# Eight small stages of an attention layer as one stage

## The chip, the cores and the metric

One core of one Trainium2 chip runs the whole program in one launch. The time is that of the device in microseconds (us): 6660.32, the median of three runs (6659.06 to 6661.24). Engines: TensorE (PE), VectorE (DVE), ScalarE (ACT), GpSimd (POOL), and SyncE (SP), which here only issues DMAs.

## The reference, cut to what matters

The program is a network of eight layers over 3125 nodes with 256 features. The change lies in the seventh, a graph layer with two paths. The attention path and the state-space ("mamba") path are both normalised and then mixed by a gate:

```
agg = segment_sum(proj[src] * attn, tgt)            # attention, 4 heads of 64
h_local = elu(agg + x + gat_b)
h_local = layer_norm(h_local, ln_local_g, ln_local_b)
y = scan(...)                                        # state space, in the order of perm
y = (y + xc * D_param) * silu(z)
y = y @ out_proj_w.T
h_attn = layer_norm(x + y[inv], ln_global_g, ln_global_b)
gate = sigmoid(h_local @ wl.T + h_attn @ wg.T)
h = gate * h_local + (1 - gate) * h_attn
```

Here `x` is the layer's normalised input. `elu(v)` is computed as `max(v, 0) + exp(min(v, 0)) - 1`.

## The kernel before, in words

**Sizes.** 3200 padded nodes are NT = 25 tiles of P = 128 rows, in NG = 5 groups of G = 5. D = 256 is KD = 2 halves of 128. Buffers with nodes on the partitions ("rows") are [128, 25, 256]; buffers with features on the partitions ("turned") are [128, 2, 3200], worked on in NCH = 8 chunks of CH = 400 nodes. All is float32. A buffer of rows has 3.28 MB (3200 KB).

**Stages.** The program is a sequence of stages. Each is a `Phase` (L53): it takes semaphores and buffers, has one program per engine, and ends with a barrier of all engines that clears its semaphores (L87). Nothing of the next stage is issued before it. Within a stage each engine's program is in order; a `wait_ge` holds everything behind it on that engine. SP's DMAs go through one queue.

**Around the change** (`attention_layer`, L3290). After `mamba_and_attention`, whose VectorE does the scan, the scan's output stands turned in `k.t` (buffer `t_sb`), the attention's sums in `k.ag` (buffer `y_sb`, 260 columns per tile, the last four the sums of the weights), the layer's input in DRAM. Then come, each a stage:

1. `gz`, `gate_rows` (L2293): SP loads the kept rows into `x_sb`, then z chunk by chunk through two buffers; ScalarE applies Silu, VectorE multiplies into `k.t`.
2. `tm`, `transform` with mode "rows" (L1147): ScalarE copies a tile of `k.t`, TensorE multiplies by `out_proj_w`, VectorE evacuates, SP stores to the DRAM table `ys`. G buffers each.
3. `lr`, `local_rows` (L2355): a chain of eight operations on one partition, with an Exp of ScalarE and a product of TensorE in it, gives a small number per tile that is added to the sums; then reciprocal, scaling, the two additions (input, `gat_b`) and elu, each as one instruction over all 6400 columns (the scaling one per head).
4. `nl`, `affine_norm` (L2156): statistics, mean and root; then three VectorE operations per tile (subtract and scale, times gain, plus bias). SP reloads a kept buffer meanwhile.
5. `tl`, `turn` (L2217): VectorE copies a tile, TensorE transposes both halves, ScalarE copies out of PSUM to the turned buffer.
6. `fr`, `fetch_rows` (L2328): GpSimd gathers rows of `ys` by the inverse permutation (`k.rank`), five buffers; VectorE copies the index, and adds the kept rows.
7. `ng`: `affine_norm` again, 8. `tt`: `turn` again, into `t2`.

The gate stage `gf` (`gate_and_feed`, L2412) then loads its weights and works on `k.t` and `t2` in chunks. It isn't touched, nor is what comes after, but for `affine_norm` of the last norm (`n2g`), which loses two options that it doesn't use.

## Time and profile before

| | us |
|---|---|
| median of 3 runs | 6660.32 |
| the profiled execution, its time | 6658.88 |
| the same, span in the trace | 6657.1 |
| TensorE matmul busy in the span | 5195.0 (78%) |
| VectorE busy | 3514.9 (53%) |
| ScalarE busy | 2499.8 (38%) |
| GpSimd busy | 1679.7 (25%) |
| mean granted clock of TensorE | 0.877 of full |

Shares are of the whole span, over stages with quite different limits; what a change to one stage is worth is read from that stage. The time is 1.8 us more than the span: the launch around it. A row of a timeline gives a group's start and length from the span's start, the engine, the line, the operation with its output and inputs, and in brackets how long the engine was idle before it and what ended that.

### The profile page before, as it was taken

To read this page: it belongs to the slowest core of one execution; us is meant where nothing else is said; L and a number is where in the kernel's file an instruction comes from. 1 tells how busy PE (TensorE), PEld (TensorE's weight loads), DVE (VectorE), ACT (ScalarE), POOL (GpSimd) and SP (SyncE) were. 2 spreads that over 40 slices of the span, in tenths; PEclk is the share of its full clock that TensorE was granted. 3 is DMA by queue.
4 is the path that set the end of the run, shared out by engine and by line. 5 is a ranking of instruction groups with operands and counts; after the bars stand their busy time and mean duration, and the time that the engine had idled before them with its cause. 6 is when DMAs were issued, how large, how long until landed. Compare 5 with 4: busy or idle time off the path is not lost. (4 is left out here: it accounts for less than half of the span.)

```text
span 6657.1 us, 91573 instructions
## 1 busy us (share of the span) xinstructions
PE 5195.0 (78%) x22747; PEld 3550.6 (53%) x22748; DVE 3514.9 (53%) x7704; ACT 2499.8 (38%) x5918; POOL 1679.7 (25%) x1614
## 2 busy tenths in 40 slices
PE   6939998999796999998999497674756666326886
PEld 3516664444584777766788375463334444213476
DVE  9837777778553444443000334324489999664111
ACT  7947774666230000002223000232456565311343
POOL 5877770000011000001111300144334444010012
PEclk9979998999798999998999799786767777668888
DMA  1113333333363222220356421365234444310055
GB/s 30 23 20 99 102 101 111 151 150 152 114 198 90 70 71 70 73 63 30 112 188 197 131 71 38 102 198 164 68 95 134 135 134 135 84 47 2 26 153 170
DMA packets 407368, 682.81 MB, mean 103 GB/s; under 512 B 72610, under 2 KB 304813, under 8 KB 406573
## 3 DMA queue, kind: packets, MB, share of 16 engines
q1 hardware_dynamic: 328684, 490.20, 22.9%
q0 software_dynamic: 74016, 186.25, 10.3%
q10 hardware_dynamic: 4512, 4.46, 0.2%
q8 instruction: 78, 1.28, 0.1%
q14 instruction: 78, 0.63, 0.0%
HBM read 511.42 MB, written 169.02 MB: 102 GB/s over the span
## 5 line engine op out<-in xcount | busy, mean ns | idle before, releaser
L1784 POOL DMA_INDIRECT e_xb<-table,source x188 | 180.7, 961 | 2383.7 <-issue 1925.1
L1099 DVE TENSOR_TENSOR a_diff<-a_cu 128x640 f32<-128x640 uint16 x480 | 396.2, 825 | 628.0 <-PE a_pa L1137 628.0
L995 PE MATMUL ty_pc<-ty_ohr,ty_ohl 128*128 128x512 bf16 (+1 forms) x3416 | 661.2, 357 | 2.5 <-DVE ty_ohl L934 2.5
L2629 POOL DMA_INDIRECT mx_at_rows<-heads,mx_at_ix x416 | 483.6, 1162 | 617.4 <-PE mx_at_pa L2675 514.6
L1137 PE MATMUL a_pa<-a_diff,y_sb 128*128 128x320 f32 (+1 forms) x2000 | 549.0, 435 | 63.4 <-DVE a_diff L1106 63.4
L1762 DVE TENSOR_TENSOR e_ys<-e_py,e_bl 128x256 f32<-128x256 f32 x188 | 79.9, 425 | 970.4 <-PE e_py L1711 970.4
L1741 ACT ACTIVATE e_h<-e_phid,e_b 128x256 f32<-128x256 f32 (+1 forms) x760 | 333.1, 438 | 689.0 <-PE e_phid L1699 671.6
L969 ACT CAST ty_new<-ty_pc 128x512 uint16<-128x512 f32 x854 | 449.8, 542 | 265.2 <-PE ty_pc L995 265.2
L1699 PE MATMUL e_phid<-e_xt,e_w 128*128 128x256 f32 (+1 forms) x2800 | 526.2, 346 | 2.9 <-ACT e_xt L1729 2.9
L1711 PE MATMUL e_py<-e_wl,e_h 128*128 128x256 f32 x2288 | 512.4, 379 | 0.0
L995 PEld LDWEIGHTS ty_pc<-ty_ohr,ty_ohl 128*128 128x128 bf16 x3416 | 314.0, 98 | 349.8 <-DVE ty_ohl L934 4.2
L1137 PEld LDWEIGHTS a_pa<-a_diff,y_sb 128*128 128x128 f32 (+1 forms) x2000 | 379.6, 191 | 225.9 <-DVE a_diff L1106 63.8
L1699 PEld LDWEIGHTS e_phid<-e_xt,e_w 128*128 128x128 f32 x2800 | 464.1, 194 | 54.1 <-issue 4.9
L1068 ACT COPY t_sb<-a_pa 128x320 f32<-128x320 f32 x80 | 34.1, 426 | 1146.5 <-PE a_pa L1137 1140.3
L2675 PE MATMUL mx_at_pa<-mx_at_rows,mx_at_oh 128*128 128x260 f32 x832 | 298.2, 481 | 206.4 <-DVE y_sb L2613 145.9
L1711 PEld LDWEIGHTS e_py<-e_wl,e_h 128*128 128x128 f32 x2288 | 424.9, 190 | 55.4 <-ACT e_h L1741 0.4
L748 POOL DMA_INDIRECT a_rows<-table,a_ix x416 | 403.6, 970 | 153.4 <-issue 121.6
L2696 ACT ACTIVATE mx_at_rows<-mx_at_rows 128x64 f32<-128x64 f32 x1664 | 406.9, 334 | 0.0
L815 PEld LDWEIGHTS a_pa<-a_oh,a_rows 128*128 128x128 f32 x1664 | 249.1, 193 | 200.2 <-issue 187.3
L1137 PE MATMUL a_pa<-a_diff,a_xs 128*128 128x320 f32 (+1 forms) x1000 | 276.6, 436 | 98.9 <-DVE a_diff L1106 98.9
L235 PE MATMUL a_ss_sums<-a_ss_tiles,a_ss_lanes 125*128 125x416 f32 x800 | 348.1, 516 | 6.3 <-ACT a_ss_tiles L228 6.3
L333 POOL DMA_INDIRECT rec<-es_recs,es_tgt x240 | 312.2, 1301 | 131.6 <-issue 130.7
(611 smaller groups left out, 8992.4 us busy)
## 6 DMA issues: line engine op xcount, KB each, us to landing
counts<-ty_snap SPq DMA_DIRECT2D x122, 800.0 KB, 3.3
a_cu<-counts SPq DMA_DIRECT2D x500, 160.0 KB, 2.2
mx_work<-bc SPq DMA_DIRECT2D x160, 320.0 KB, 3.6
e_w<-in_L_ffn_W SPq DMA_DIRECT2D x33, 1024.0 KB
e_wl<-in_L_ffn_W SPq DMA_DIRECT2D x32, 1024.0 KB, 7.9
e_wl<-in_L_ffn_Wd SPq DMA_DIRECT2D x32, 1024.0 KB, 5.7
ybuf<-e_ys POOLq DMA_DIRECT2D x78, 256.0 KB
e_w<-in_L_ffn_w SPq DMA_DIRECT2D x16, 1024.0 KB
```

Source lines behind the costliest of these rows:

```text
L235: mm = pe.matmul(self.sums[:, 0:ST], self.lanes[:, b, j, :], self.tiles[:, b, j, :], start=False, stop=False)
L333: g.indirect_dma_start(rec, bass.IndirectOffsetOnAxis(ap=tgt[:, c:c + 1], axis=0), recs[:, c, :], None).then_inc(placed[c // HALF % 2].sem ...
L748: g.indirect_dma_start(rows[:, j, :], None, table, bass.IndirectOffsetOnAxis(ap=ix[:, j:j + 1], axis=0)).then_inc(landed[j].sem, 16)
L969: a.copy(new[:, u % 2, q * WIDE:q * WIDE + w], pc[:, q, 0:w]).then_inc(taken, 1)
L995: mm = pe.matmul(pc[:, q, 0:w], ohl[:, h, j, ts(q, P)], ohr[:, h, j, 0:w], start=j == 0, stop=j == ROWS - 1)
L1099: v.tensor_tensor(diff[:, m % DIFFS, :], cu[:, s % R, :], cu[:, (s - 1) % R, :], ALU.subtract).then_inc(done, 1)
L1137: mm = pe.matmul(pa[:, q, 0:H], xs[l % 2][0:rows, s, ts(q // 2, P)], diff[0:rows, m % DIFFS, ts(q % 2, H)], start=s == 0, stop=s == NT - 1)
L1699: mm = pe.matmul(phid[:, (offs[l] + f) % NB, 0:size], ws[l][:, sl, q, f * P:(f + 1) * P], src, start=q == 0, stop=q == kt - 1)
L1711: mm = pe.matmul(py[:, (s * NR + n) % 2, 0:D], hs[-1][:, q, n * P:(n + 1) * P], wls[:, s, q, :], start=q == 0, stop=q == KL - 1)
L1741: a.activation(hs[l][:, f, :], phid[:, (offs[l] + f) % NB, 0:size], hidden[l][2], bias=bs[l][:, sl, f:f + 1]).then_inc(hact, 1)
L2629: g.indirect_dma_start(self.rows[:, h * STEP + j, :], None, self.table, bass.IndirectOffsetOnAxis(ap=self.ix[:, h, j:j + 1], axis=0)).then ...
L2696: ins = a.activation(part, part, ACT.Identity, scale=self.rows[:, j, D + q:D + q + 1])
```

## The change

The eight stages become one, `join_paths`, written out without loops. What each engine does in it:

- **SP** loads z through three buffers, then `out_proj_w`; it stores projected tiles as they come, and issues the load of the kept rows in five groups once the last z load and fifteen stores are issued. The other kept buffer is reloaded last.
- **VectorE** does the small chain, then the eight products with z with the scaling of the attention's sums (per group of five tiles) between them; then the additions and elu per group, with the statistics of each group at once; the subtraction and scaling of the first norm in place; then per fetched tile the addition and the statistics; then the second norm. Gain and bias are not applied here.
- **TensorE** multiplies straight from `k.t` (no copy), two PSUM buffers; transposes straight from the normalised rows in pairs of tiles, four PSUM buffers.
- **ScalarE** does Silu, evacuates the projection into five buffers, computes for elu `Relu(-v)` and `Exp(-that)` per group, the roots, and writes the transposed halves to `k.t` and `t2` with `Identity`, gain as scale and bias as bias, from two [128, 1] columns in SBUF: a turned row has its feature on the partition.
- **GpSimd** loads the small vectors, waits for all stores, then gathers with ten buffers and takes its index from `k.rank` directly.

```
+def join_paths(nc, k, w, lists, zs, kept, ys, refill, t2):
+    F, own, ZR, RG, SLOTS = D // HEADS, lists[3], 3, 10, 4
+    groups = [slice(g * G, g * G + G) for g in range(NG)]
+    pairs = [range(t, min(t + 2, NT)) for t in range(0, NT, 2)]
+    rows, held = k.rows, k.x
+        begun, risen, powered, told, chain, scaled = (ph.sem(n) for n in ("begun", "risen", "powered", "told", "chain", "scaled"))
+        bb, inv, low = ph.sb("bb", [P, D]), ph.sb("inv", [P, NT, HEADS]), ph.sb("low", [P, 2, G, D])
+        z, wsb, out = ph.sb("z", [P, ZR, KD, CH]), ph.sb("w", [P, KD, D]), ph.sb("out", [P, G, D])
+        fetched, st = ph.sb("fetched", [P, RG, D]), ph.sb("st", [P, NT, 6])
+        pb, pz, pt = ph.ps("pb", [P, 512]), ph.ps("pz", [P, 2, 512]), ph.ps("pt", [P, SLOTS, 2, KD, P])
...
             @b.sync
             def _(sp):
+                for c in range(ZR):
+                    sp.dma_start(z[:, c, :, :], zs[:, :, c * CH:(c + 1) * CH]).then_inc(zld[c], 16)
+                sp.dma_start(wsb[:, :, :], w("out_proj_w").rearrange("(k p) n -> p k n", p=P)).then_inc(wld, 16)
+
+                def store(tiles):
+                    for t in tiles:
+                        sp.wait_ge(put, t + 1)
+                        sp.dma_start(ys[ts(t, P), :], out[:, t % G, :]).then_inc(stored[t % G], 16)
+
+                ends = [max(c - ZR + 1, 0) * CH // P for c in range(NCH)]
+                for c in range(ZR, NCH):
+                    sp.wait_ge(mixed, c - ZR + 1)
+                    sp.dma_start(z[:, c % ZR, :, :], zs[:, :, c * CH:(c + 1) * CH]).then_inc(zld[c % ZR], 16)
+                    store(range(ends[c - 1], ends[c]))
+                for g, s in enumerate(groups):
+                    sp.dma_start(held[:, s, :], kept[:, s, :]).then_inc(yld[g], 16)
+                store(range(ends[-1], NT))
+                sp.wait_ge(scaled, NG)
+                sp.dma_start(k.y, refill).then_inc(refilled, 16)
+                sp.wait_ge(refilled, 16)
...
+            @b.gpsimd
...
+                for s in stored:
+                    g.wait_ge(s, 16 * NG)
+                for t in range(NT):
+                    if t >= RG:
+                        g.wait_ge(attended, t - RG + 1)
+                    g.indirect_dma_start(fetched[:, t % RG, :], None, ys, bass.IndirectOffsetOnAxis(ap=k.rank[:, t:t + 1], axis=0)).then_inc(landed[t % RG].sem, 16)
...
             @b.vector
...
+                def mix(i):
+                    v.wait_ge(silu, i + 1)
+                    part = k.t[:, :, i * CH:(i + 1) * CH]
+                    v.tensor_tensor(part, part, z[:, i % ZR, :, :], ALU.mult).then_inc(mixed, 1)
+
+                def share(g):
+                    s = groups[g]
+                    v.tensor_tensor(rows[:, s, :].rearrange("p t (h f) -> p t h f", h=HEADS), k.ag[:, s, 0:D].rearrange("p t (h f) -> p t h f", h=HEADS),
+                                    inv[:, s, :].unsqueeze(3).broadcast_to([P, G, HEADS, F]), ALU.mult).then_inc(scaled, 1)
+
+                def local(g):
+                    s = groups[g]
+                    v.wait_ge(scaled, g + 1)
+                    v.wait_ge(yld[g], 16)
+                    c(v.tensor_tensor(rows[:, s, :], rows[:, s, :], held[:, s, :], ALU.add))
+                    v.tensor_tensor(rows[:, s, :], rows[:, s, :], bb[:, :].unsqueeze(1).broadcast_to([P, G, D]), ALU.add).then_inc(biased, 1)
+
+                def bend(g):
+                    s = groups[g]
+                    v.wait_ge(bent, g + 1)
+                    v.wait_ge(biased, g + 1)
+                    c(v.scalar_tensor_tensor(rows[:, s, :], rows[:, s, :], 0.0, low[:, g % 2, :, :], ALU.max, ALU.add))
+                    v.tensor_scalar(rows[:, s, :], rows[:, s, :], -1.0, None, ALU.add).then_inc(joined, 1)
+                    v.wait_ge(joined, g + 1)
+                    for t in range(g * G, g * G + G):
+                        v.bn_stats(st[:, t, :], rows[:, t, :]).then_inc(stats, 1)
+
+                def spreads(n):
...
+                    v.sem_inc(varied, 1)
+                    v.wait_ge(rooted, n + 1)
+                    c(v.reciprocal(rstd[:, n, :], rstd[:, n, :]))
+
+                def even(n, buf):
+                    for t in range(NT):
+                        v.tensor_scalar(buf[:, t, :], buf[:, t, :], mean[:, n, t:t + 1], rstd[:, n, t:t + 1], ALU.subtract, ALU.mult).then_inc(evened, 1)
+
                 v.wait_ge(told, 1)
+                c = Chain(v, chain)
+                mix(0)
+                c(v.tensor_tensor(inv[:, :, :], k.ag[:, :, D:D + HEADS], spread(pb[:, 0:NT], HEADS), ALU.add))
                 c(v.reciprocal(inv[:, :, :], inv[:, :, :]))
+                for i in range(1, NCH):
+                    mix(i)
+                    if i <= NG:
+                        share(i - 1)
+                v.wait_ge(vld, 16 * 5)
+                for g in range(NG):
+                    local(g)
+                    if g:
+                        bend(g - 1)
+                bend(NG - 1)
+                spreads(0)
+                even(0, rows)
+                for t in range(NT):
+                    landed[t % RG].wait(v, 16 * (t // RG + 1))
+                    v.tensor_tensor(held[:, t, :], held[:, t, :], fetched[:, t % RG, :], ALU.add).then_inc(attended, 1)
+                    v.wait_ge(attended, t + 1)
+                    v.bn_stats(st[:, t, :], held[:, t, :]).then_inc(stats, 1)
+                spreads(1)
+                even(1, held)
...
             @b.tensor
...
+                pe.wait_ge(wld, 16)
+                for t in range(NT):
+                    pe.wait_ge(mixed, (t * P + P - 1) // CH + 1)
+                    if t >= 2:
+                        pe.wait_ge(put, t - 1)
+                    for q in range(KD):
+                        mm = pe.matmul(pz[:, t % 2, 0:D], k.t[:, q, ts(t, P)], wsb[:, q, :], start=q == 0, stop=q == KD - 1)
+                    mm.then_inc(mul, 1)
+                for n, buf in enumerate((rows, held)):
+                    for m, tiles in enumerate(pairs):
+                        i = n * len(pairs) + m
+                        pe.wait_ge(evened, n * NT + tiles[-1] + 1)
+                        if i >= SLOTS:
+                            pe.wait_ge(evac, KD * (i - SLOTS + 1))
+                        for j, t in enumerate(tiles):
+                            for q in range(KD):
+                                mm = pe.transpose(pt[:, i % SLOTS, j, q, :], buf[:, t, ts(q, P)], k.ident[:, :])
+                        mm.then_inc(tdone, 1)
...
             @b.scalar
...
+                def bright(i):
+                    a.wait_ge(zld[i % ZR], 16 * (i // ZR + 1))
+                    a.activation(z[:, i % ZR, :, :], z[:, i % ZR, :, :], ACT.Silu).then_inc(silu, 1)
+
+                def take(t):
+                    a.wait_ge(mul, t + 1)
+                    if t >= G:
+                        a.wait_ge(stored[t % G], 16 * (t // G))
+                    a.copy(out[:, t % G, :], pz[:, t % 2, 0:D]).then_inc(put, 1)
+
+                done = 0
+                for i in range(NCH):
+                    bright(i)
+                    for t in range(done, i * CH // P):
+                        take(t)
+                    done = max(done, i * CH // P)
+                for t in range(done, NT):
+                    take(t)
+                for g, s in enumerate(groups):
+                    a.wait_ge(biased, g + 1)
+                    if g >= 2:
+                        a.wait_ge(joined, g - 1)
+                    a.activation(low[:, g % 2, :, :], rows[:, s, :], ACT.Relu, scale=-1.0).then_inc(negated, 1)
+                    a.wait_ge(negated, g + 1)
+                    a.activation(low[:, g % 2, :, :], low[:, g % 2, :, :], ACT.Exp, scale=-1.0).then_inc(bent, 1)
+                for n, dest in enumerate((k.t, t2)):
+                    a.wait_ge(varied, n + 1)
+                    a.activation(rstd[:, n, :], var[:, n, :], ACT.Sqrt).then_inc(rooted, 1)
+                    a.wait_ge(vld, 16 * 5)
+                    for m, tiles in enumerate(pairs):
+                        i = n * len(pairs) + m
+                        a.wait_ge(tdone, i + 1)
+                        for q in range(KD):
+                            cols = dest[:, q, tiles[0] * P:(tiles[-1] + 1) * P].rearrange("p (t c) -> p t c", c=P)
+                            a.activation(cols, pt[:, i % SLOTS, 0:len(tiles), q, :], ACT.Identity, scale=gains[:, n, q:q + 1], bias=biases[:, n, q:q + 1]).then_inc(evac, 1)
...
-        gate_rows(nc, k, zs, y_kept)
-        transform(nc, "tm", k, k.t, w("out_proj_w"), "rows", table=ys)
-        k.x, k.y = k.y, k.x
-        k.rows = sb("rows", [P, NT, D])
-        local_rows(nc, k, by_dst, w("gat_b"))
-        affine_norm(nc, "nl", k, k.rows, w("ln_local_g"), w("ln_local_b"), k.rows, False, refill=x_kept)
-        turn(nc, "tl", k, k.t, rows=k.rows)
-        fetch_rows(nc, k, ys)
-        affine_norm(nc, "ng", k, k.rows, w("ln_global_g"), w("ln_global_b"), k.rows, False)
         with nc.sbuf_tensor("t2", [P, KD, NP], F32) as t2:
-            turn(nc, "tt", k, t2, rows=k.rows)
+            with nc.sbuf_tensor("rows", [P, NT, D], F32) as k.rows:
+                join_paths(nc, k, w, by_dst, zs, y_kept, ys, x_kept, t2)
+            k.x, k.y = k.y, k.x
             gate_and_feed(nc, k, t2, w("wl"), w("wg"), w("ff1_w"), w("ff1_b"), w("ff2_w"), w("ff2_b"))
         turn_back(nc, "tb", k, k.t, k.y)
-        affine_norm(nc, "n2g", k, k.y, w("ln2_g"), w("ln2_b"), k.x, True)
+        affine_norm(nc, "n2g", k, k.y, w("ln2_g"), w("ln2_b"), k.x)
...
-_L3_BY_PARTITION = ("conv_b", "dt_proj_b", "D_param", "ff1_b", "ff2_b")
+_L3_BY_PARTITION = ("ln_local_g", "ln_local_b", "ln_global_g", "ln_global_b", "conv_b", "dt_proj_b", "D_param", "ff1_b", "ff2_b")
```

The small chain at the start of VectorE's program, left out above, is that of `local_rows` (L2372 to L2382). The statistics in `spreads` are those of `affine_norm` (L2181 to L2187).

## Rows read from the trace of the kernel before

**Rows 1.** Table of windows: length, each engine's busy us (instructions), clock, DMA share, GB/s.
```profile
5704.10:5953.60 249.50, 41.03 (x202) 35.77 (x202) 158.25 (x373) 46.48 (x93) 23.64 (x25) 0.58 0.21 69
...
5739.50:5769.50 30.00, 23.91 (x100) 20.43 (x100) 10.62 (x25) 9.74 (x25) 0.00 (x0) 0.88 0.34 118
```

**Rows 2.** Timeline at the stretch's start: start, us, engine, line, operation.
```profile
5703.64 0.43 DVE L2613 TENSOR_TENSOR y_sb<-y_sb,mx_at_pa 128x260 f32 x1 [0.21 <-PE mx_at_pa L2675]
5705.18 0.34 SPq L2309 DMA_DIRECT2D x_sb<-y_kept  x1
```

**Rows 3.** Timeline of the stage `lr` (local_rows).
```profile
5770.05 0.19 DVE L2372 CAST lr_first<-d_own 1x52 f32<-1x52 int32 x1 [3.06 <-PEq L87]
...
5776.20 0.22 ACT L2407 ACTIVATE lr_gap<-lr_gap 1x25 f32<-1x25 f32 x1 [4.90 <-DVE lr_gap L2379]
...
5777.47 0.26 DVE L2385 TENSOR_TENSOR lr_inv<-y_sb,lr_pb 128x100 f32<-128x100 f32 x1 [0.77 <-PE lr_pb L2402]
...
5778.57 7.03 DVE L2388 TENSOR_TENSOR rows<-y_sb,lr_inv 128x1600 f32<-128x1600 f32 x4
...
5792.50 6.83 DVE L2393 TENSOR_TENSOR rows<-rows,lr_bb 128x6400 f32<-128x6400 f32 x1
5799.36 3.49 DVE L2394 TENSOR_SCALAR lr_low<-rows 128x6400 f32<-128x6400 f32 x1
5802.89 5.54 ACT L2409 ACTIVATE lr_low<-lr_low 128x6400 f32<-128x6400 f32 x1 [26.47 <-DVE lr_low L2394]
```

**Rows 4.** The tile gz_z, by line: ns min/median/max.
```profile
L2305 ACT ACTIVATE gz_z<-gz_z x8: 869/869/870, 5716.8 to 5736.8; 128x800 f32<-128x800 f32 x8
L2325 DVE TENSOR_TENSOR t_sb<-t_sb,gz_z x8: 991/993/993, 5717.8 to 5737.8; 128x800 f32 x8
```

**Rows 5.** Timeline of the stage `tm` (transform, "rows").
```profile
5742.61 23.91 PE L1202 MATMUL tm_pz<-tm_w,tm_ast 128*128 128x256 f32 x100 [39.13 <-DMA tm_w<-in_L_gnn_out_proj_w]
...
5744.80 0.42 DVE L1226 COPY tm_out<-tm_pz 128x256 f32<-128x256 f32 x1 [6.03 <-PE tm_pz L1202]
```

**Rows 6.** A window of 2 us in the stage `nl`, columns as rows 1.
```profile
5826.00:5828.00 2.00, 0.00 (x0) 0.00 (x0) 2.00 (x7) 0.00 (x0) 0.00 (x0) 0.50 0.98 422
```

**Rows 7.** Timeline: statistics of `nl`; straight code of a refresh stage.
```profile
5820.31 8.27 DVE L2177 BATCH_NORM_STATS2 nl_st<-rows  x25 [1.42 <-PEq L87]
...
4492.90 0.17 DVE L1977 TENSOR_TENSOR c_mean<-c_st 128x5 f32<-128x5 f32 x1
...
4494.91 1.71 DVE L1968 TENSOR_SCALAR y_sb<-x_sb,c_mean,c_rstd 128x256 f32<-128x256 f32 x5
```

**Rows 8.** Timeline of the stage `fr` (fetch_rows), then its gathers by tile.
```profile
5869.92 0.94 POOL L2341 DMA_INDIRECT fr_rows<-ys,fr_ix  x1 [195.89 <-DVE fr_ix L2346]
...
5872.84 0.42 DVE L2350 TENSOR_TENSOR rows<-fr_rows,x_sb 128x256 f32 x1 [3.53 <-DMA fr_rows<-ys,fr_ix]
5873.41 0.15 DVE L2352 COPY fr_ix<-rank 128x1 uint32 x1
...
L2341 POOL DMA_INDIRECT fr_rows<-ys,fr_ix x25: 942/946/947, 5869.9 to 5899.9; - x25
```

**Rows 9.** Timeline of `tt` and `gf`, then two tiles of `gf`.
```profile
5943.36 7.12 PE L2250 MATMUL tt_pt<-ident,tt_stage 128*128 128x128 f32 x40 [76.06 <-DVE tt_stage L2238]
5944.19 8.51 ACT L2258 COPY t<-tt_pt 128x256 f32 x25 [29.30 <-PE tt_pt L2250]
...
5953.56 0.38 SPq L2427 DMA_DIRECT2D gf_wl<-in_L_gnn_wl  x1
...
5966.54 1.28 ACT L2471 ACT_TABLE_LOAD   x1 [13.85 <-PE gf_pg L2440]
...
L2477 ACT ACTIVATE gf_hid<-gf_ph,gf_b x32: 594/595/595, 5974.7 to 6092.1; 128x400 f32<-128x400 f32 x32
...
L2471 ACT ACTIVATE gf_gate<-gf_pg x16: 504/504/505, 5967.8 to 6081.3; 128x400 f32<-128x400 f32 x16
```

**Rows 10.** From the page's groups, the attention's gathers beside VectorE's scan.
```profile
L2629 POOL DMA_INDIRECT mx_at_rows<-heads,mx_at_ix x416 | 483.6, 1162 | 617.4 <-PE mx_at_pa L2675 514.6
```

More of the change, by code:

```diff
@@ L2153, in _, with affine_norm @@
                 a.activation(var[:, :], var[:, :], ACT.Sqrt).then_inc(root, 1)
-def affine_norm(nc, name, k, src, gain, bias, dest, add, eps=1e-5, refill=None):
+def affine_norm(nc, name, k, src, gain, bias, dest, eps=1e-5):
     with Phase(nc, name) as ph:
         ld, dve, root = ph.sem("ld", "hardware"), ph.sem("dve"), ph.sem("root")
-        filled = ph.sem("filled", "hardware")
         st = ph.sb("st", [P, NT, 6])
@@ L2168, in _ @@
                 sp.dma_start(bb[:, :], bias.partition_broadcast(P)).then_inc(ld, 16)
-                if refill is not None:
-                    sp.dma_start(k.x, refill).then_inc(filled, 16)
-                    sp.wait_ge(filled, 16)
             @b.vector
@@ L2190, in _ @@
                 v.wait_ge(ld, 32)
-                n, m = c.n, 4 if add else 3
+                n, m = c.n, 4
                 with v.Fori(0, NG) as i:
@@ L2386, in _ @@
                 c(v.reciprocal(inv[:, :, :], inv[:, :, :]))
-                for h in range(HEADS):
-                    v.tensor_tensor(k.rows[:, :, h * F:(h + 1) * F], ag[:, :, h * F:(h + 1) * F], spread(inv[:, :, h], F), ALU.mult).then_inc(dve, 1)
-                c.n += HEADS
-                v.wait_ge(dve, c.n)
-                c(v.tensor_tensor(k.rows[:, :, :], k.rows[:, :, :], k.y[:, :, :], ALU.add))
-                v.wait_ge(ld, 16)
-                c(v.tensor_tensor(k.rows[:, :, :], k.rows[:, :, :], bb[:, :].unsqueeze(1).broadcast_to([P, NT, D]), ALU.add))
@@ L2394, in _ @@
-                c(v.tensor_scalar(low[:, :, :], k.rows[:, :, :], 0.0, None, ALU.min))
-                v.wait_ge(act, 1)
-                c(v.scalar_tensor_tensor(k.rows[:, :, :], k.rows[:, :, :], 0.0, low[:, :, :], ALU.max, ALU.add))
-                c(v.tensor_scalar(k.rows[:, :, :], k.rows[:, :, :], -1.0, None, ALU.add))
+                for i in range(1, NCH):
[3 more added lines that the diff above has]
+                v.wait_ge(vld, 16 * 5)
```

227 lines of the change are left out of this document (28 added, 199 removed).

## The prediction

> **What bounds the kernel now.** I read the table of windows first, then the timeline of the stretch, then single tiles. The eight stages that the change merges run from the end of VectorE's last scan operation (5703.64 + 0.43 = 5704.07) to the first DMA of the gate stage at 5953.56: 249.5 us [rows 1, 2, 9]. In them VectorE works 158.3 us, ScalarE 46.5, TensorE 41.0, GpSimd 23.6 [rows 1]; their sum is 269 us, hardly more than the stretch, so the engines take turns. No wait between two neighbouring stages can be hidden, as each stage ends in a barrier. The rest of the kernel (gate stage, last norm) isn't touched, so the question is how long one merged stage takes. I lay it out along VectorE, with time zero at its release, 1.1 us after 5704.07 (SP's first DMA came at 5705.18, [rows 2]).
>
> **The change part by part, along VectorE.**
>
> *Opening, to 10.7.* The small chain on the softmax's tops stays: 5770.05 to 5777.47, 7.4 us [rows 3]. Z's first load now goes ahead of the 3.2 MB of kept rows and has landed by then. But ScalarE is in order: its Exp stood at +6.15 (5776.20), then comes the table load for Silu, 1.28, and a Silu of 0.87 [rows 3, 4, 9]. So the first product starts at 8.6 (1.2 us late), takes 1.0, and the inverse of the sums 1.1 (5777.47 to 5778.57) [rows 3, 4].
>
> *Eight products with z, five shares, projection beside them, to 30.6.* VectorE alone would need 7 x 1.03 + 5 x 1.5 = 14.7 (a share is 1280 elements; the four old ones had 1600 in 1.76 each [rows 3]), to 25.4. I don't think it gets that. ScalarE's program places three evacuations between one Silu and the next, and each waits for TensorE: the old projection took 23.91 us for 25 tiles, the first of them out after 2.2 (5742.61 to 5744.80), so 0.9 each after it [rows 5]. First product done 9.7, first tile 11.9, two more at the clock that TensorE has after idling (mean 0.88 of full over that old stage [rows 1]) 14.7, evacuation 0.4, the third Silu ends at 16.0. Then five rounds of 3 x 0.9 bring the eighth Silu to 29.5 and its product to 30.6. What the old stage paid for copying the operand (25 ScalarE copies) and VectorE's evacuations vanish from VectorE.
>
> *Local rows, to 73.4.* Per group of five tiles: two additions of 1280 elements, 1.5 each (6400 took 6.83), then the maximum-add 1.5, the minus one 0.8 (6400 took 3.49), and five statistics of 0.33 with a wait, 1.8: 3.0 + 4.1 [rows 3, 7]. That is 35.5 for five groups. The separate minimum of 3.49 and the 5.54 of Exp that VectorE waited for [rows 3] go. What is late next is ScalarE again: the first bend needs Relu and Exp, and they are queued behind the last seven evacuations. SP puts five loads of kept rows (3.28 MB) into its queue at about 26, ahead of the stores of tiles 15 to 24. At 422 GB/s [rows 6] they take 7.8 us and, with some 2 us of latency, a store behind them lands at about 36.5. The ring of five output buffers makes evacuation 20 wait for store 15, so the last evacuation ends at 40.0; Relu 1.25 (a fifth of 5.54 and a start), table 1.28, Exp 1.25 make 43.9. VectorE, through with two groups' additions at 36.7, stands for 7.2 us. From there five bends (20.5) and three pairs of additions (9.0) bring it to 73.4. If stores were not held the wait would be 3.5, that is 3.7 less.
>
> *First norm, to 85.1.* From the last statistics to the scaling takes 2.1 in straight code (4492.90 to 4494.91, and 0.1 for the semaphore ahead), plus a table load for Sqrt, 1.3, which I take as exposed; at most that is gained. Then 25 subtract-and-scale operations at 0.33 (five in 1.71, each 0.41, overlapping) are 8.3 [rows 7]. The multiplications by gain and additions of bias, 50 VectorE operations, and 25 copies into a stage are gone. Transposes and ScalarE's 26 turned evacuations (13 us, below) lie beside the next loop.
>
> *Fetched rows, to 107.6.* The index copies go. Per tile: addition, its semaphore and the next start 0.57 (5872.84 to 5873.41), statistics 0.33: 0.90, 22.5 in all [rows 7, 8]. GpSimd issues a gather each 1.25 (5869.9 to 5899.9 in 24 steps, 0.946 of it busy) [rows 8], 2.9 from its start to VectorE's use. All 25 stores have landed by 42 to 44, and the first ten gathers are out 12.5 later, long before 85.1. The other fifteen wait for freed buffers: the last starts at 85.7 + 14 x 1.25 = 103.2 and is usable at 106.1, and VectorE gets to it at 106.7. It is nearly a tie; bounds of the loop are 18.8 (0.75 a tile, if the semaphore's time is hidden) and 31.3 (all gathers at GpSimd's pace).
>
> A rule of the Trainium skill bears on this (SBUF — State Buffer, "SBUF: two separate sides"): while VectorE holds the port pair that it shares with GpSimd, GpSimd cannot write its descriptors. The trace has gathers of 1162 ns beside a busy VectorE against 946 in the old fetch stage [rows 8, 10], so it shows a slowing by a quarter and no full block. By the rows a gather beside the bends costs 1.5 with its gap, ten 15 us, still hidden; by the rule as a full block they would start only in VectorE's gaps (a rival, below).
>
> *Second norm and the tail, to 124.0.* 2.1 again, no new table. Then VectorE runs 8.3, TensorE turns pairs of tiles (40 transposes in 7.12, 0.18 each, 0.72 a pair) and ScalarE writes them with gain and bias. This last one is dearer than the copy that it replaces. 25 old copies took 8.51, 0.34 each [rows 9]. A bias from memory cost 0.595 - 0.504 = 0.09 on the same shape [rows 9]; with a scale from memory too I take 0.17, which gives 0.5 each, 1.0 a pair (bounds: 0.34 if it's free, 0.6). So ScalarE is the bound: first pair after 1.5, twelve full pairs and a single tile 12.8, together 14.3. Exit to the gate stage 0.9 (5952.70 to 5953.56) [rows 9].
>
> *Off the path:* the vectors on GpSimd's queue (due at 30), the refill of 3.2 MB on SP after the last store (landed by 52), the first norm's transposes. Without cover the refill would cost 10 us.
>
> A second rule of the skill speaks against the change (ScalarE: Activation LUTs, "What ACT_TABLE_LOAD costs"): a load of 1283 ns is followed by a drain of 1380 ns. The trace has a load at 5966.54 for 1.28 and the first Sigmoid at 5967.8 [rows 9], so no drain. With it, the three loads that I count as exposed (Silu, Exp, Sqrt) would make the time about 4 us longer, 6541.
>
> **Sum.** 1.1 + 124.0 + 0.9 = 126.0 against 249.5: 123.5 less. The profiled execution had a span of 6657.1 and a time of 6658.88, so 6658.88 - 123.5 = 6535.4 in its terms. The median shown is 6660.32, 1.4 above it: 6536.8, given as 6537.
>
> **Rivals.**
> 1. *ScalarE never holds VectorE.* Products done at 25.4, rows at 60.9, norm at 72.8 (with 3.4 and 8.3), loop 95.3, then 2.1 and a tail of 10.9 with ScalarE at 0.34: 108.3, or 110.3 with the ends. Time 6660.3 - 139.2 = 6521. For it: ScalarE has only 46 us of work before. Against: evacuations and Silus stand in one order.
> 2. *Gathers become the bound.* If GpSimd gets no gather out before the loop (blocked by VectorE's wide operations, or the stores late by 40 us), the loop is 25 gathers at 1.25 to 1.46, 31 to 36.5, in place of 22.5: 9 to 14 longer, 6546 to 6551. Against: rows 10.
> 3. *TensorE stays at 1.2 GHz*, as it stands beside these stages (0.50 in [rows 6]), where I count on 2.4 GHz after the first tiles. A tile then takes 1.9: five rounds of 5.7 instead of 2.7, and seven tiles at the end 7 us more, less the hold by the stores (already over, 3.7): 15 + 7 - 3.7 = 18, 6555. Against: the old projection climbed within a few tiles once it ran without a pause [rows 1, 5].
> 4. *Slower than before: straight code.* The old stages were loops over five groups; the new one has some 185 VectorE operations written out. If each had to wait for its code, all of it would lie on the path; it decides from 123.5 / 185 = 0.67 us per operation, and at 0.75 the time is 6537 + 139 = 6676. Against: another straight stage runs five such operations in 1.71 [rows 7].
>
> **Chances.** My forecast 0.58 (own range 6528 to 6546), rival 1 0.13, rival 2 0.12, rival 3 0.09, rival 4 0.02; 0.06 for sums of small misses outside these. Same to within 0.2% (13 us, what a measurement of this kernel can tell) would need a stage of over 236 us: 0.01. Faster 0.97. The range takes in the forecast, the edge of rival 1 and rivals 2 and 3: 6522 to 6556.
>
> **What the changed profile would show.** The merged stage 126 us long. VectorE waiting for Silus some 5 us in all, one wait of about 7 for ScalarE before the first maximum-add, and nearly none for gathers. If it waits for DMA in the fetch loop, my tie fell the wrong way. ScalarE's turned evacuations at 0.5 us apart and bounding the end; if they are at 0.34, the tail is 3 to 4 shorter. A granted clock under 0.6 during the projection would be rival 3. The gate stage must take as long as before; if it doesn't, the prediction is wrong in a part that I left out.

## The result, and the profile after

The changed kernel takes 6541.20 us (median of four runs, 6540.17 to 6542.21) against 6660.78 for the one before: 119.6 us less, a ratio of 0.9819 (95% interval 0.9802 to 0.9837). The prediction was 6537, with a range of 6522 to 6556. The profiled execution took 6542.21, its span is 6540.4. Between the two profiled executions the span fell by 116.7 us (6657.1 to 6540.4): the merged stage gives 119.1, what stands ahead of it took 4.2 more (the scan ends at 5708.27, before at 5704.07), and what follows took 1.8 less. The gate stage itself, from its first DMA to the last norm's, is as long as before: 158.0 against 157.8.

The first view is the timeline of the merged stage, where it begins and ends (the rest of each line as in [rows 2]). The last VectorE operation of the scan ends at 5707.84 + 0.43 = 5708.27, the gate stage's first DMA is at 5838.71: 130.4 us, against 249.5 before [rows 1, 2, 9] and 126.0 forecast.

```profile
5707.84 0.43 DVE L2554 TENSOR_TENSOR y_sb<-y_sb,mx_at_pa 128x260 f32 x1 [0.21 <-PE mx_at_pa L2616]
5709.39 1.97 SPq L2170 DMA_DIRECT2D jp_z<-zs  x3
...
5715.59 0.22 ACT L2314 ACTIVATE jp_gap<-jp_gap 1x25 f32<-1x25 f32 x1 [10.40 <-DVE jp_gap L2213]
5715.83 1.28 ACT L2318 ACT_TABLE_LOAD   x1
...
5718.10 0.99 DVE L2221 TENSOR_TENSOR t_sb<-t_sb,jp_z 128x800 f32<-128x800 f32 x1 [2.01 <-ACT jp_z L2318]
```

```profile
5838.71 0.38 SPq L2368 DMA_DIRECT2D gf_wl<-in_L_gnn_wl  x1
```

The opening is as forecast: Exp, then the table load, then Silu, and the first product 8.7 after the release at 5709.39 (8.6 forecast). Compare [rows 2, 3].

The second view is the timeline from the last rounds, where ScalarE evacuates the projection between two Silus, to the first maximum-add.

```profile
5733.35 0.37 ACT L2324 COPY jp_out<-jp_pz 128x256 f32<-128x256 f32 x1 [1.54 <-DMA ys<-jp_out]
...
5736.79 3.12 SPq L2184 DMA_DIRECT2D x_sb<-y_kept  x5
...
5739.05 0.37 ACT L2324 COPY jp_out<-jp_pz 128x256 f32<-128x256 f32 x1 [0.91 <-DMA ys<-jp_out]
...
5739.96 16.83 SPq L2176 DMA_DIRECT2D ys<-jp_out  x10
...
5743.18 1.49 DVE L2232 TENSOR_TENSOR rows<-rows,x_sb 128x1280 f32<-128x1280 f32 x1 [1.97 <-DMA x_sb<-y_kept]
...
5750.92 0.71 ACT L2324 COPY jp_out<-jp_pz 128x256 f32<-128x256 f32 x2 [9.85 <-DMA ys<-jp_out]
...
5751.43 4.33 PE L2298 MATMUL jp_pz<-jp_w,t_sb 128*128 128x256 f32 x12 [8.88 <-ACT jp_out L2324]
5753.51 0.37 ACT L2324 COPY jp_out<-jp_pz 128x256 f32<-128x256 f32 x1 [1.88 <-PE jp_pz L2298]
...
5756.07 1.27 ACT L2338 ACTIVATE jp_low<-rows 128x1280 f32<-128x1280 f32 x1
...
5757.36 1.28 ACT L2340 ACT_TABLE_LOAD   x1
5758.65 1.27 ACT L2340 ACTIVATE jp_low<-jp_low 128x1280 f32<-128x1280 f32 x1
...
5759.95 1.49 DVE L2239 SCALAR_TENSOR_TENSOR rows<-rows,jp_low 128x1280 f32<-128x1280 f32 x1 [10.83 <-ACT jp_low L2340]
5760.29 2.14 POOL L2201 DMA_INDIRECT jp_fetched<-ys,rank  x1 [0.30 <-issue]
```

The reader is to see three things. Two evacuations (5733.35 and 5739.05) wait for a store, and then the first addition (5743.18) 1.97 us for kept rows. Evacuation 20 waits 9.85 us for the store of tile 15, which SP issued at 5739.96, behind the five loads of kept rows (5736.79). And VectorE stands 10.83 us before its first maximum-add, until ScalarE, behind its evacuations, is through with Relu (5756.07), a table load and Exp. The gathers run beside that (5760.29) and are told of below.

The third view is the rest of the stage, by the same columns: first norm, fetch loop, second norm and tail. It answers to [rows 7 to 9].

```profile
5783.59 1.28 ACT L2343 ACT_TABLE_LOAD   x1
...
5790.69 0.23 ACT L2343 ACTIVATE jp_rstd<-jp_var 128x25 f32<-128x25 f32 x1 [5.82 <-DVEq L2255]
...
5791.30 8.17 DVE L2261 TENSOR_SCALAR rows<-rows,jp_mean,jp_rstd 128x256 f32<-128x256 f32 x25
...
5799.37 0.43 DVE L2282 TENSOR_TENSOR x_sb<-x_sb,jp_fetched 128x256 f32<-128x256 f32 x1
...
5800.18 0.41 DVE L2282 TENSOR_TENSOR x_sb<-x_sb,jp_fetched 128x256 f32<-128x256 f32 x1
...
5815.97 0.43 DVE L2282 TENSOR_TENSOR x_sb<-x_sb,jp_fetched 128x256 f32<-128x256 f32 x1 [0.36 <-DMA jp_fetched<-ys,rank]
...
5817.16 0.42 DVE L2282 TENSOR_TENSOR x_sb<-x_sb,jp_fetched 128x256 f32<-128x256 f32 x1 [0.31 <-DMA jp_fetched<-ys,rank]
...
5824.07 8.17 DVE L2261 TENSOR_SCALAR x_sb<-x_sb,jp_mean,jp_rstd 128x256 f32<-128x256 f32 x25
...
5826.07 11.73 ACT L2350 ACTIVATE t<-jp_pt,jp_biases,jp_gains 128x256 f32<-128x256 f32 x26 [2.39 <-PE jp_pt L2308]
```

The scaling of 25 tiles takes 8.17. The fetch loop from 5799.37 to 5821.79 takes 22.4: 0.81 for its first tile (5799.37 to 5800.18), then 0.79 a tile, and 1.2 to 1.3 for the last six (5815.97 to 5817.16 is one), where each addition waits for its gather. ScalarE's 26 turned instructions take 11.73, 0.45 each, and end at 5837.80, where VectorE is through at 5832.24: ScalarE bounds the end, as forecast.

### The profile page after: what moved, and what is told of

Read it like the earlier page. It is cut to its first block and busy times, and to the rows that moved or that the text cites. A ratio compares the mean times of both kernels' runs of the same rounds, so it can differ in the third digit from the quotient of the medians.

```text
span 6540.4 us, 90176 instructions
## 1 busy us (share of the span) xinstructions
PE 5198.6 (79%) x22747; PEld 3549.0 (54%) x22748; DVE 3445.6 (53%) x7515; ACT 2507.4 (38%) x5926; POOL 1683.8 (26%) x1619
```

## The experiments

For all but e6 I compare the length of the merged stage, from the end of the scan's last VectorE operation to the gate stage's first DMA: the stages ahead of it are the same instructions in all these kernels, and yet the merged stage began up to 8.5 us apart (at 5705.91 in e5, at 5714.44 in e3), so that the time alone can't tell 2 us. Each length is that of one profiled execution. The change has 130.4, and 130.2 in a later run on another chip (e11); no other measure of the stage's own noise was taken. e1 to e4 ran on one chip, e5 to e8 on a second, e9 to e11 on a third.

### e1: ten output buffers

```
-        ph.sems("stored", G, "hardware")
+        ph.sems("stored", OUTS, "hardware")     # OUTS = 10
...
-        ph.sb("out", [P, G, D])
+        ph.sb("out", [P, OUTS, D])
```

> Ten output buffers instead of five between the projection's evacuations and their stores, nothing else. In the changed kernel the merged stage takes 130.4 us and VectorE waits 10.8 us for the first Exp. Theory A: ScalarE is held at evacuation 20 because its buffer's store stands behind the five loads of kept rows in SP's queue. With ten buffers evacuations 20 to 24 need only stores issued ahead of the loads; ScalarE is through by about 38 us into the stage instead of 47.9, the wait shrinks to 1 or less, the stage to 120 to 121, the time to 6531. Theory B: the wait is made by ScalarE's own Relu, table load and Exp (3.9 us) and by the late kept rows: then it stays at 7 or more and the time at 6538 to 6541.

Measured: stage 119.3 (5712.31 to 5831.6), time 6535.25 (6530.31 to 6538.88). Timeline of e1, evacuations and the first maximum-add:

```profile
5745.95 1.49 DVE L2233 TENSOR_TENSOR rows<-rows,x_sb 128x1280 f32<-128x1280 f32 x1 [1.61 <-DMA x_sb<-y_kept]
...
5748.32 0.37 ACT L2325 COPY jp_out<-jp_pz 128x256 f32<-128x256 f32 x1 [0.49 <-PE jp_pz L2299]
...
5752.89 1.49 DVE L2240 SCALAR_TENSOR_TENSOR rows<-rows,jp_low 128x1280 f32<-128x1280 f32 x1 [0.99 <-ACT jp_low L2341]
```

The last evacuation starts at 5748.32, 36.0 after the scan's end (47.5 in the change), and VectorE's wait is 0.99 in place of 10.83. Theory A holds, B falls: of the 10.8 nearly all was the ring of five buffers behind the queue's order. The time came out 4 above the forecast 6531; in the profiled execution the merged stage began 4.0 us later than the change's.

### e2: the stores ahead of the kept rows

```
-                for g, s in enumerate(groups):
-                    sp.dma_start(held[:, s, :], kept[:, s, :]).then_inc(yld[g], 16)
                 store(range(ends[-1], NT))
+                for g, s in enumerate(groups):
+                    sp.dma_start(held[:, s, :], kept[:, s, :]).then_inc(yld[g], 16)
```

> SP issues the stores of tiles 15 to 24 ahead of the five loads of kept rows, nothing else. Theory A (place in SP's queue): evacuations run on, the wait before the first maximum-add goes, but the first addition now waits for kept rows issued some 8 us later, so VectorE gains 10.8 and loses 5 to 8: stage 125 to 128, time 6536 to 6539. Theory C (the DMA engines are simply full from the projection on, so the order makes no difference): stage 130, time 6541.

Measured: stage 128.3 (5707.56 to 5835.9), time 6542.30. Timeline of e2:

```profile
5745.58 2.74 SPq L2185 DMA_DIRECT2D x_sb<-y_kept  x5
...
5750.16 1.49 DVE L2232 TENSOR_TENSOR rows<-rows,x_sb 128x1280 f32<-128x1280 f32 x1 [10.23 <-DMA x_sb<-y_kept]
...
5757.10 1.49 DVE L2239 SCALAR_TENSOR_TENSOR rows<-rows,jp_low 128x1280 f32<-128x1280 f32 x1 [0.99 <-ACT jp_low L2340]
```

The wait before the maximum-add falls to 0.99 here too, and 10.23 of waiting stand before the first addition instead, where A had put 5 to 8. A holds in kind: the order of SP's queue decides which of two waits VectorE has. By itself it saves 2 us of the stage, and nothing that the time shows (6542.30 against 6541.20).

### e3: fifteen gather buffers

```
-    F, own, ZR, RG, SLOTS = D // HEADS, lists[3], 3, 10, 4
+    F, own, ZR, RG, SLOTS = D // HEADS, lists[3], 3, 15, 4
```

> Fifteen buffers for gathered rows instead of ten, nothing else. If the last six tiles of the fetch loop are paced by GpSimd (1.22 apart instead of 0.79), five more gathers ahead of the loop bring it from 22.4 us to 19.8 and the time to 6538.5. If those waits come from the DMAs' own time to land, or VectorE's rate falls where GpSimd works beside it, the loop stays at 22 and the time at 6541.

Measured: stage 127.9 (5714.44 to 5842.3), time 6544.36; the stage began 6 us later than in the change, so the gain doesn't show in the time, and the forecast 6538.5 was missed. The 25 additions by tile, first in e3, then in the change (the two times are the starts of the first and the last):

```profile
L2282 DVE TENSOR_TENSOR x_sb<-x_sb,jp_fetched x25: 406/408/416, 5805.6 to 5824.5; 128x256 f32<-128x256 f32 x25
```

```profile
L2282 DVE TENSOR_TENSOR x_sb<-x_sb,jp_fetched x25: 406/409/431, 5799.4 to 5820.9; 128x256 f32<-128x256 f32 x25
```

That is 18.9 us from first to last, 0.79 a tile throughout, against 21.5. GpSimd's pace made the slow tiles.

### e4: a plain copy out of PSUM

```
-  a.activation(cols, pt[:, i % SLOTS, 0:len(tiles), q, :], ACT.Identity, scale=gains[:, n, q:q + 1], bias=biases[:, n, q:q + 1]).then_inc(evac, 1)
+  a.activation(cols, pt[:, i % SLOTS, 0:len(tiles), q, :], ACT.Copy).then_inc(evac, 1)
```

> ScalarE writes the turned halves with a plain copy; gain and bias of both norms are left out of the computation. The question is what they cost there. If the two columns from memory make it (0.45 us apart against 0.34 for the copies before the change), the tail after the second norm falls from 13.7 us to about 10.8 and the time by 3 to 6538. If TensorE's transposes or PSUM pace the tail, spacing and time stay within 1 us.

Measured: stage 126.9 (5706.91 to 5833.8), 3.5 less; time 6539.33. ScalarE's rows of the tail:

```profile
5824.49 1.45 ACT L2350 ACTIVATE t<-jp_pt 128x256 f32<-128x256 f32 x4 [2.38 <-PE jp_pt L2308]
...
5827.84 5.03 ACT L2350 ACTIVATE t<-jp_pt 128x256 f32<-128x256 f32 x18 [0.20 <-PE jp_pt L2308]
```

Eighteen take 5.03, 0.28 each, against 0.45 with two columns: the two columns cost 0.17, as taken. The copy in this form costs less than the old turning stage's 0.34 [rows 9]. The tail is 10.4 us long (13.7), 3.3 of the 3.5.

### e5 and e6: each part alone

e5 is the changed kernel with the weights of both norms on VectorE as rows, and with e4's plain copy:

```
+                        for j, t in enumerate(tiles):
+                            v.wait_ge(scl, at + j + 1)
+                            v.tensor_tensor(buf[:, t, :], buf[:, t, :], gains[:, n, :], ALU.mult).then_inc(scl, 1)
+                        for j, t in enumerate(tiles):
+                            v.wait_ge(scl, at + G + j + 1)
+                            v.tensor_tensor(buf[:, t, :], buf[:, t, :], biases[:, n, :], ALU.add).then_inc(evened, 1)
```

> The merged stage with the norms' gain and bias applied on VectorE as rows, as before the change (two operations more per tile, 100 in all, at 0.335), and plain copies out of PSUM: the merging alone, without the second part. 33.5 us more on VectorE's line, 3 to 5 less in the tail, since ScalarE now keeps ahead: stage 159 to 162, time 6570 to 6573. Rival: the 50 operations of the first norm are partly hidden because the fetched rows would have been waited for anyway (six short waits, 2 us in all): 6568.

Measured: stage 160.4 (5705.91 to 5866.3), 30.0 more than the change; time 6570.52 against 6658.02 for the kernel before, 87.5 less. No part of the 50 operations was hidden: the six short waits for gathers stayed.

e6 is the kernel before, eight stages, with the weights in `turn` and no multiplications and additions in the norms:

```
+                            for q in range(KD):
+                                a.activation(dest[:, q, ds((i * G + j) * P, P)], pt[:, j, q * P:(q + 1) * P], ACT.Identity, scale=cols[:, 0, q:q + 1], bias=cols[:, 1, q:q + 1]).then_inc(evac[j], 1)
```

> The kernel before with its eight stages, but gain and bias applied by ScalarE when the turned halves leave PSUM (two instructions of 128 columns per tile in place of one copy of 256): the second part alone. Each norm loses 50 VectorE operations at 0.335, 16.8 us; each turning stage grows from 0.33 to about 0.65 a tile, 8 us. Twice 8.8: 17 to 18 less, 6643. If the ScalarE instructions overlap better (0.25 each), 25 less, 6635. If the gain were lost in the turning stages, 6655 to 6660.

Measured: 6642.46 against 6658.02, ratio 0.9975 (0.9965 to 0.9984), 15.6 less; the stretch of eight stages 234.3 (249.5). Its first turning stage:

```profile
5845.83 17.55 ACT L2274 ACTIVATE t_sb<-tl_pt,tl_cols 128x128 f32 x50 [12.98 <-DMA tl_cols<-in_L_gnn_ln_local_b]
```

It has 50 instructions in 17.55, 0.35 each, where 25 copies took 8.5 [rows 9]. The first norm is over 17.4 us sooner, but this turning stage is 10.2 longer, and 1.0 of that is ScalarE's wait for the two columns, which are loaded at the stage's start (it begins 2.1 after VectorE, 1.2 in the kernel before): more than half of what VectorE saves is lost again, since nothing else runs in that stage. In the merged stage the same move is worth 30.0, for the first norm's instructions lie beside the fetch loop there, pairs of tiles make them half as many, and the columns have long been loaded.

### e7: all loads first

z goes into `t2`, unused until the second norm, so that nothing has to be freed for it:

```
+                for c in range(NCH):
+                    sp.dma_start(t2[:, :, part], zs[:, :, part]).then_inc(zld[c], 16)
...
+                for g, s in enumerate(groups):
+                    sp.dma_start(held[:, s, :], kept[:, s, :]).then_inc(yld[g], 16)
+                store(range(NT))
```

> All eight loads of z (into the still unused turned buffer t2) and then the kept rows are issued at the start of the merged stage; five output buffers as in the change. Theory D: in the change the DMA engines are nearly full during the projection (busy share 0.77 over it, 0.97 in its middle), which holds single evacuations and then the stores. With the loads done before the first stores (6.6 MB by about 16 to 18 us into the stage) no evacuation waits for a store after that, the first addition does not wait, and VectorE's wait for Exp is that of ScalarE alone: seven evacuations 6.2, Relu, table, Exp 3.9, less two groups' additions 6.0, about 4. Stage 119 to 121, time 6530 to 6532. Rival: early evacuations now wait for stores behind the loads, 3 to 5 us, and the stage comes to 124.

Measured: stage 125.9 (5708.15 to 5834.0), time 6536.72 (the median of three executions; a fourth took 12669.82, and why stays open). The rival was right in kind; it had a wait of 3 to 5 and a stage of 124. Timeline of e7:

```profile
5721.59 31.07 SPq L2180 DMA_DIRECT2D ys<-jp_out  x25
...
5731.98 0.37 ACT L2322 COPY jp_out<-jp_pz 128x256 f32<-128x256 f32 x1 [5.67 <-DMA ys<-jp_out]
...
5733.15 0.99 DVE L2218 TENSOR_TENSOR t_sb<-t_sb,t 128x800 f32<-128x800 f32 x1 [5.37 <-ACT t L2316]
...
5755.12 1.49 DVE L2236 SCALAR_TENSOR_TENSOR rows<-rows,jp_low 128x1280 f32<-128x1280 f32 x1 [2.27 <-ACT jp_low L2338]
```

Evacuation 5 waits 5.67 us for the store of tile 0, issued at 5721.59 behind 6.6 MB of loads, and VectorE's fourth product 5.37 for the Silu behind it. Here 6.6 MB of loads stood ahead of a store, in the change 3.3 MB, and both times the ring of five stopped.

### e8: the reordered version

e7's loads, ten output and fifteen gather buffers, and on ScalarE another order (`bright` is a Silu, `take` an evacuation, `curve` a group's Relu and Exp):

```
+                for i in range(NCH):
+                    bright(i)
+                    if i in (3, 5, 7):
+                        for t in range((i - 3) // 2 * 2, (i - 3) // 2 * 2 + 2):
+                            take(t)
+                for t in range(6, 18):
+                    take(t)
+                curve(0)
+                for t in range(18, 21):
+                    take(t)
+                curve(1)
+                for t in range(21, NT):
+                    take(t)
+                for g in range(2, NG):
+                    curve(g)
```

> All of it: loads first with z in t2, ten output buffers, fifteen gather buffers, and on ScalarE nearly all Silus ahead of the evacuations (two of them after the fourth, sixth and eighth Silu), Relu and Exp of the first group after evacuation 17 and of the second after 20. VectorE's line: 8.7, product and inverse 2.1, products and shares 14.7 without waiting to 25.5, additions of two groups 6.0, bends and additions 29.1 with at most 1 to 2 of waiting, norm 2.3 + 8.2, loop 19.8, 2.3, tail 13.7: 107 to 110, ends 2: stage 109 to 112, time 6520 to 6523. If TensorE's evacuations keep ScalarE from Relu and Exp in time (rival), VectorE waits 4 to 6 us more: 6526.

Measured: stage 110.2 (5706.02 to 5816.2), time 6520.79 (6520.50 to 6523.69), ratio to before 0.9793. One wait for ScalarE stays, of 2.92; the forecast had 1 to 2:

```profile
5736.16 1.27 ACT L2330 ACTIVATE jp_low<-rows 128x1280 f32<-128x1280 f32 x1
5737.45 1.28 ACT L2332 ACT_TABLE_LOAD   x1
5738.75 1.27 ACT L2332 ACTIVATE jp_low<-jp_low 128x1280 f32<-128x1280 f32 x1
...
5740.05 1.49 DVE L2237 SCALAR_TENSOR_TENSOR rows<-rows,jp_low 128x1280 f32<-128x1280 f32 x1 [2.92 <-ACT jp_low L2332]
```

### e9: is it the load of the queue?

On another chip, with e10 and the change again (e11): there the kernel before takes 6898.46, and the stages ahead of this one are longer in all of them, but the change's merged stage is 130.2 (5944.20 to 6074.4). e9 is set beside that one.

```
                 for c in range(ZR, NCH):
                     sp.wait_ge(mixed, c - ZR + 1)
-                    sp.dma_start(z[:, c % ZR, :, :], zs[:, :, c * CH:(c + 1) * CH]).then_inc(zld[c % ZR], 16)
```

> The changed kernel with only the first three chunks of z loaded; chunks 3 to 7 use what stands in the three buffers, so their values are left out of the computation. SP's order, its waits and all stores stay. Theory D: in the change z loads (400 KB) and stores (3 x 128 KB) of one round fill the DMA engines (busy share 0.97 in the middle), so a backlog holds evacuations 11 and 17 for 1.5 and 0.9 us and puts the kept rows and the stores behind them late (first addition waits 2.0, store 15 lands 11 us after its issue). With 2 MB less in the queue the two holds and the first addition's wait vanish and store 15 lands within 9: the wait before the first maximum-add falls from 10.8 to 8 or less and the stage from 130.4 to 124 to 127. Rival: the holds come from the stores' own way to DRAM (latency), not from the load of the queue: then they stay, and the stage is within 1.5 of 130.4.

Measured: stage 128.8 (5944.97 to 6073.8), time 6778.60 (one execution). The views are e9's timeline around the hold, two lines of e11's, e9's DMA windows (columns as [rows 1]), and three windows of the change in its first run.

```profile
5977.44 1.49 DVE L2231 TENSOR_TENSOR rows<-rows,x_sb 128x1280 f32<-128x1280 f32 x1 [0.77 <-DMA x_sb<-y_kept]
...
5984.84 0.71 ACT L2325 COPY jp_out<-jp_pz 128x256 f32<-128x256 f32 x2 [8.24 <-DMA ys<-jp_out]
...
5995.02 1.55 DVE L2238 SCALAR_TENSOR_TENSOR rows<-rows,jp_low 128x1280 f32<-128x1280 f32 x1 [11.63 <-ACT jp_low L2341]
```

```profile
5986.40 0.71 ACT L2324 COPY jp_out<-jp_pz 128x256 f32<-128x256 f32 x2 [9.49 <-DMA ys<-jp_out]
...
5995.68 1.55 DVE L2239 SCALAR_TENSOR_TENSOR rows<-rows,jp_low 128x1280 f32<-128x1280 f32 x1 [11.10 <-ACT jp_low L2340]
```

```profile
5956.00:5972.00 16.00, 16.00 (x62) 12.97 (x63) 12.05 (x11) 8.05 (x19) 0.00 (x0) 0.86 0.32 107
5976.00:5978.00 2.00, 2.00 (x9) 1.44 (x8) 1.23 (x2) 0.37 (x1) 0.00 (x0) 1.00 1.02 420
```

```profile
5729.00:5734.00 5.00, 4.36 (x21) 3.35 (x20) 3.98 (x4) 2.54 (x7) 0.00 (x0) 1.00 0.97 276
5736.80:5750.90 14.10, 5.74 (x25) 4.02 (x23) 7.98 (x7) 2.78 (x7) 0.00 (x0) 0.88 0.92 325
5751.40:5756.20 4.80, 4.33 (x12) 3.28 (x12) 0.00 (x0) 1.38 (x5) 0.00 (x0) 0.68 0.27 88
```

All short holds of the rounds are gone (two in the change, three in e11), with the DMA engines at 0.32 busy over the rounds and 0.47 in their middle (5966 to 5971); the change has 0.97 there. The first addition still waits, 0.77 for e11's 1.58. The long hold is 8.24 (9.49), and the wait before the maximum-add is not shorter but longer, 11.63 (11.10), as VectorE came there 2.0 earlier. Store 15, issued at 5975.40, frees its buffer at 5984.84, 12.3 after the first load of kept rows (5972.57), against 13.7 in e11 and 14.1 in the change's first run (5736.79 to 5750.92). So the backlog of z and stores makes the short holds and 1.4 to 1.9 us of the long one; the rest is there without it. From the first kept row to the hold's end e9 moves 329 GB/s, with no z in the queue, and the change 325.

Counted from the scan's end, evacuation 20 starts 2.3 us sooner than in e11, but the last evacuation ends only 1.4 sooner. Between them lie the last matmuls: in e9 TensorE was granted 0.50 for all of them (1.2 GHz, 5984.9 to 5990.0), in e11 the clock rose within them (0.77 from 5990 to 5991, then 1.00). That gave back 0.9. Theory D holds for the small part alone, and its forecast of 124 to 127 was missed: it put down to the backlog what was the loads' own. The rival had the stage within 1.5 of 130.4, which it misses by 0.1, and its short holds did not stay.

### e10 and e11: a further step, beside the change

e10 is e8 with Relu and Exp of the first group two evacuations earlier, and with the last two pairs of the tail, four instructions, written by VectorE (`LATE = 2 * len(pairs) - 2`). Its edit against e8:

```
-                for t in range(6, 18):
+                for t in range(6, 16):
                     take(t)
                 curve(0)
-                for t in range(18, 21):
+                for t in range(16, 21):
                     take(t)
...
+                for i in range(LATE, 2 * len(pairs)):
...
+                        v.tensor_scalar(cols, pt[:, i % SLOTS, 0:len(tiles), q, :], gains[:, 1, q:q + 1], biases[:, 1, q:q + 1], ALU.mult, ALU.add).then_inc(late, 1)
```

> The reordered version with two more edits: Relu and Exp of the first group already after evacuation 15, and the last two pairs of turned tiles (a full one and the single tile) written by VectorE, which is idle by then. First edit: VectorE's wait of 2.9 before the first maximum-add falls to about 1. Second: ScalarE's tail is 4 instructions of 26 shorter, 1.6 us. Stage 110.2 to 106 to 107, time 6517. Rival: the evacuations put off by the first edit hold TensorE, and the second group's Relu and Exp come late in turn, so that only the tail is gained: 108.5.

> The changed kernel once more, on the same chip and in the same rounds as the version above, so that the two can be set beside each other: stage 130.4, time 6538 to 6545. The stages ahead of the merged one have differed by up to 10 us between executions of kernels that are alike there, so the time of one kernel on another chip may differ by as much; the stage's length should not.

Measured on the chip of e9: e10 6754.65 (6754.03 to 6757.52), the change 6778.21 (6770.02 to 6783.45), before 6898.46. The stage is 107.7 (5948.19 to 6055.9) against 130.2. Timeline of e10, the two waits that are left before the maximum-adds:

```profile
5980.50 1.49 DVE L2238 SCALAR_TENSOR_TENSOR rows<-rows,jp_low 128x1280 f32<-128x1280 f32 x1 [1.20 <-ACT jp_low L2339]
...
5988.24 1.49 DVE L2238 SCALAR_TENSOR_TENSOR rows<-rows,jp_low 128x1280 f32<-128x1280 f32 x1 [0.70 <-ACT jp_low L2339]
```

Most of the first wait went (1.20 for 2.92), and 0.70 of it came back at the second group, as the rival had it in small; the tail gave the rest, 1.6. The stage is 2.5 shorter than e8's on another chip; the forecast was 106 to 107. This version beats both kernels: 0.979 of before (0.9777 to 0.9804), where the change has 0.9823 on that chip.

## Why the prediction came out

The mechanism was right in the main: one merged stage on VectorE's line, with ScalarE's order, and not VectorE's work, deciding its first half. Two things came right by luck: the fetch loop's sum, and part of the total, in which a step 6.2 too short meets later ones 1.8 too long. In the profiled executions the stage shrank by 119.1 where 123.5 was forecast. The first four rows are times after the release, the others lengths; all in us:

| step | forecast | measured |
|---|---|---|
| first product starts | 8.6 | 8.7 |
| eighth product done | 30.6 | 31.8 |
| two groups' additions done | 36.7 | 39.7 |
| last evacuation done | 40.0 | 46.8 |
| wait before the first maximum-add | 7.2 | 10.8 |
| local rows done, after the release (bends and additions: 29.5, measured 29.1) | 73.4 | 79.6 |
| first norm: statistics, root, 25 scalings | 11.7 | 10.4 |
| fetch loop | 22.5 | 22.4 |
| second norm's statistics | 2.1 | 2.3 |
| tail | 14.3 | 13.7 |

**The term that was too small** is DMA time. I let the kept rows and the store behind them land at 36.5, from 422 GB/s in [rows 6], one large load alone. Evacuation 20 came free at 41.5. Of these 5.0, 1.4 are the loads' issue (27.4 after the release where I had about 26; 26.5 in e9, so 0.9 of it is the short hold in the rounds), and 1.4 to 1.9 the backlog (e9, on another chip). What is left, about 2, comes by subtraction and lies with the kept rows and the stores themselves, which together move 325 GB/s (329 in e9), not 422. That is a mean: the change moves 412 from 5742 to 5744 and 259 from 5748 to 5750. No run separates what the stores and what the five loads take of it. A second size in that step: TensorE, idle for 8.88 behind the hold, was granted 0.68 after it (window from 5751.4; 0.50, that is 1.2 GHz, to 5754, and 1.00 from 5755), where it had 1.00 in the rounds, and from the end of the hold to the last evacuation it took 5.25 (5750.92 to 5756.17), not 3.5. Together 6.8, of which 6.2 were left when the local rows were done. The first addition's 1.97 cost nothing: VectorE was early for the maximum-add. The waits for Silus sum to 7.1 us where I had some 5.

**The table load before the root** was free: it stands at 5783.59, while ScalarE was idle, ahead of the wait (Sqrt at 5790.69; the norm came out 1.3 shorter). Only Silu's and the first Exp's are exposed. No drain follows a load: 5757.36 + 1.28 = 5758.64, and Exp starts at 5758.65. So the Trainium skill's 1380 ns after a load (ScalarE: Activation LUTs, "What ACT_TABLE_LOAD costs") don't show here either. With that drain the prediction had 6541, which is the time measured; that agreement is chance, as no drain is there and the missing 4 us are those of the term above, less what later terms had too much.

**The fetch loop** came out right by two errors. VectorE takes 0.79 a tile, not 0.90: the time of the semaphore between addition and statistics, which I had counted, is hidden. So it caught up with GpSimd, and six tiles went at GpSimd's 1.25. My near tie fell the other way, and e3 shows what that costs: 2.5.

**Rivals.** The first (ScalarE never holds VectorE) is what e8 builds; its 110.3 us for the stage is e8's 110.2, but by chance: e8 has the dearer tail, a faster loop and still a wait of 2.92 for ScalarE, and the rival's sum has a slip (60.9 + 3.4 + 8.3 is 72.6, not 72.8). The second did not occur: the ten gathers beside the bends took 0.94 to 2.14 us and were issued by 5773.3, 26 us ahead of their first use. So no gather had to wait for the end of VectorE's work. Whether single VectorE instructions held one, as the Trainium skill has it (SBUF — State Buffer, "SBUF: two separate sides"), these lengths don't decide: gathers of 0.95 lie beside two-input additions, and the one of 2.14 beside the minus one (0.83). The third: TensorE was at 2.4 GHz through the rounds (clock 1.00 in the window above), and below it only at the start (0.52 from 5719 to 5724) and after the hold. The fourth (code) is out: 25 scalings, written out, in 8.17.

**The two parts.** e5 and e6 measure them apart: merging alone 87.5, weights alone 15.6, both 119.6. The sum of the two is 103; the weights are worth 30 in the merged stage.

## What to carry to other kernels

When stages are merged, write down for each in-order engine, ScalarE and the DMA queue above all, what now stands ahead of each thing that another engine waits for; the longest engine's work alone (rival 1) gave 110 us for a stage that took 130. Check a ring of output buffers against the loads that can stand between two stores in the same queue: with five buffers ScalarE stood 9.85 us behind 3.3 MB, with ten it never waited for a store, and the stage was 11.1 shorter. Loads issued early into an empty queue gave 4.5 with the ring of five. Whether another engine's queue for the kept rows would do as well was not run. And moving work to another engine pays by what that engine does at that time: the same move was worth 15.6 us in stages of its own and 30.0 beside other work.

## What the runs showed that I had not expected

- Loads of 1600 B rows and stores of 1 KB rows together kept the DMA engines 0.97 busy at 276 GB/s, where a single load of rows reached 422 at 0.98 [rows 6]. The change's kept rows and stores made 325 at 0.92.
- A ScalarE instruction of 256 columns out of PSUM cost 0.28 us as a copy in a row of eighteen (e4) and 0.45 with scale and bias from memory.
- With less to wait for, TensorE's clock took part of the gain back: in e9 the hold ended 2.3 us sooner, and 0.9 of that was lost to matmuls at 1.2 GHz.
- Unchanged stages ahead of the merged one differed by up to 8.5 us between executions of different kernels, on two chips (the merged one's start between 5705.9 and 5714.4), and by 236 us on another chip (5944.20), while the change's merged stage kept its length within 0.2 us.
